# A two-layer transformer kernel on one core: new times for every piece of the schedule, and layer 1's middle rounds written out on all engines

## The reference

```python
# layer 0, attention: 16 heads of 16, rotary positions on q and k, causal mask
att = softmax(where(mask, q @ k.T / sqrt(16), -inf)); y = (att @ v) @ Wo.T + bo
# layer 0, feed forward: hidden 768, integer weights scaled by 1/127
out = (silu(x @ wg.T) * (x @ wu.T)) @ wd.T
# layer 1, attention: 16 heads of 64, clamped scores, causal mask
sim = 50 * tanh(q @ k.T / 8 / 50); y = (softmax(where(causal, sim, min)) @ v) @ Wo.T
# layer 1, channel mix: x mixed with the token before it
out = sigmoid(xr @ W_r.T) * (square(relu(xk @ W_k.T)) @ W_v.T)
```

## Time and profile before

| | us |
|---|---|
| median of 3 runs | 1533.23 |
| lowest and highest | 1530.34, 1533.83 |
| the profiled execution | 1535.46 |
| its span, first to last instruction | 1533.3 |
| PE, DVE, ACT, POOL busy in it | 1431.3, 1077.9, 800.4, 813.9 |

### The profile page before, as it was taken

How to read it: one execution, slowest core, us unless ns; L and a number is a source line. 1 busy time by engine, 2 the same in 40 slices (tenths; PEclk the granted TensorE clock), 3 DMA queues, 4 the chain that set the end, 5 groups by cost and what they waited for, 6 DMA issues and landing times. The chain is left out here.

```text
span 1533.3 us, 32896 instructions
## 1 busy us (share of the span) xinstructions
PE 1431.3 (93%) x12438; PEld 1053.3 (69%) x12438; DVE 1077.9 (70%) x2036; ACT 800.4 (52%) x1132; POOL 813.9 (53%) x1003
## 2 busy tenths in 40 slices
PE   5788989899999999999999999999999999999996
PEld 3555756667676767677777777777777777777765
DVE  7778687778887787785656658657677586675765
ACT  2443444353544443545656666665666566566651
POOL 4233434344443544344657567656666575756652
PEclk8888999899999999999999999999999999999999
DMA  5111120212121111220100001100100001000000
GB/s 189 60 59 53 48 82 22 84 43 83 41 83 41 55 55 62 78 70 16 48 29 1 1 4 40 42 1 1 43 1 15 29 1 42 1 1 29 1 29 14
DMA packets 45762, 61.32 MB, mean 40 GB/s; under 512 B 3760, under 2 KB 31312, under 8 KB 45648
## 3 DMA queue, kind: packets, MB, share of 16 engines
q1 hardware_dynamic: 44784, 59.03, 11.4%
q10 hardware_dynamic: 864, 0.66, 0.2%
HBM read 25.83 MB, written 8.39 MB: 22 GB/s over the span
## 5 line engine op out<-in xcount | busy, mean ns | idle before, releaser
L1696 ACT ACTIVATE l_probs<-psum 128x1024 f32<-128x1024 f32 (+1 forms) x192 | 164.4, 880 | 131.3 <-PE psum L1964 107.7
L912 ACT ACTIVATE l_probs<-psum 128x512 f32<-128x512 f32 x256 | 138.2, 595 | 179.0 <-PE psum L1179 176.6
L994 DVE TENSOR_REDUCE l_rowmax<-psum 128x2 f32<-128x1024 f32 (+2 forms) x192 | 159.2, 864 | 39.7 <-PE psum L1140 39.3
L310 POOL TENSOR_SCALAR_AFFINE_SELECT l_probs<-l_probs 128x256 f32<-128x256 f32 (+1 forms) x384 | 182.4, 506 | 0.0
L305 POOL TENSOR_TENSOR l_pool_holder<-expo 128x1 f32<-128x1 f32 x128 | 31.6, 247 | 282.7 <-ACT l_probs L1702 186.5
L1771 DVE TENSOR_TENSOR l_qk_lo<-psum,l_qk_hi 128x1024 fp32r<-128x1024 f32 x64 | 77.9, 1218 | 134.9 <-ACT l_qk_hi L1686 134.5
L1702 ACT ACTIVATE l_probs<-l_probs 128x2048 f32<-128x2048 f32 (+1 forms) x128 | 161.6, 1268 | 0.5
L2007 PE MATMUL psum<-l_probs,l_v 128*32 128x512 f32 (+3 forms) x2048 | 151.1, 434 | 0.7 <-DVE l_att L1793 0.7
L1780 DVE RECIPROCAL l_keysum<-psum 128x256 f32<-128x256 f32 x64 | 112.2, 1754 | 51.7 <-PE psum L1993 51.2
L1793 DVE TENSOR_TENSOR l_att<-psum,l_keysum 64x256 f32<-64x256 f32 x256 | 108.0, 422 | 20.3 <-PE psum L2007 13.0
L2007 PEld LDWEIGHTS psum<-l_probs,l_v 128*32 128x32 f32 x2048 | 64.2, 110 | 83.0 <-issue 71.4
(11 more groups left out here) (212 smaller groups left out, 4176.4 us busy)
## 6 DMA issues: line engine op xcount, KB each, us to landing
l_kT<-l_roped_hi SPq DMA_DIRECT2D x32, 256.0 KB, 2.5
l_qT<-l_roped_hi SPq DMA_DIRECT2D x32, 256.0 KB, 2.5
l_xin<-in_x SPq DMA_DIRECT2D x8, 512.0 KB, 4.4
l_kT<-l_roped_lo SPq DMA_DIRECT2D x16, 256.0 KB, 2.5
l_qT<-l_roped_lo SPq DMA_DIRECT2D x16, 256.0 KB, 2.5
l_x<-in_x SPq DMA_DIRECT2D x8, 512.0 KB, 4.0
x_mid<-l_x SPq DMA_DIRECT2D x8, 512.0 KB, 3.1
l_xin<-x_mid SPq DMA_DIRECT2D x8, 512.0 KB, 4.3
```

The source lines that it names most:

```text
L310: nc.gpsimd.affine_select(out=part, in_=part, compare_op=ALU.is_ge, fill=0.0, base=0, pattern=[[0, part.shape[1]], [1, P]], channel_multip ...
L912: space.free(nc.scalar.activation(probs[:, SLOT[p], e, c0:c1], space.unit(*use), ACT.Exp, scale=HD0 ** -0.5), *use)
L994: reduced = nc.vector.tensor_reduce(rowmax[:, a // 2, :, a % 2, t], space.unit("max", a, k)[:, :, c0:c0 + (t + 1) * P], mybir.AxisListType ...
L1696: space.free(nc.scalar.activation(probs[:, p % 2, :, c0:c1], space.unit("score", p, u)[:, :, 0:c1 - c0], ACT.Tanh, scale=HD1 ** -0.5 / CLA ...
```

## The change

Three things are changed, and no piece is added, removed or rewritten.

1. Every time in both layers' `table` and `moved_table`, in `loading_table` and in `prologue_table` is another one. The number of rounds between batches stays; the order within a round changes in places, on every engine.
2. A few banks change: in layer 0 those of `maxT`, `score`, `heat`, `warm`, `outT`, `o` and `x_T` in some indices, in layer 1 those of `end_heat`.
3. `loop()` of layer 1 is called with `unrolled=True`, so that ACT, DVE, POOL and SP also have rounds 3 to 6 written out. Layer 0 loops as before.

The core of the diff. Layer 0's loading, one moved line and one line of banks:

```diff
-        "rope_hi": {(0, 0): -20.101, (0, 1): 21.429, (0, 2): 46.819, (0, 3): 71.689, (1, 0): -15.688, (1, 1): 24.852, (1, 2): 50.682, (1, 7): 168, (2, 0): -14.54, (2, 1): 31.73, (2, 2): 54.28, (2, 7): 179.17, (3, 0): 6.041, (3, 1): 38.791, (3, 2): 56.891, (3, 7): 179.411},
+        "rope_hi": {(0, 0): -27.088, (0, 1): 22.112, (0, 2): 47.212, (0, 3): 71.998, (1, 0): -18.44, (1, 1): 25.56, (1, 2): 47.41, (1, 7): 168, (2, 0): -5.63, (2, 1): 27.82, (2, 2): 54.09, (2, 7): 173.94, (3, 0): 8.097, (3, 1): 36.997, (3, 2): 58.147, (3, 7): 178.927},
...
-        "load_lo": {(4,): -11.75, (5,): -11.68, (6,): -11.6, (7,): -7.78, (8,): -6.33, (9,): -2.17, (10,): 7.46, (11,): 12.9, (12,): 16.93, (13,): 40.62, (14,): 46.77, (15,): 52.09},
+        "load_lo": {(4,): -12.87, (5,): -12.68, (6,): -11.12, (7,): -8.66, (8,): -6.11, (9,): 2.47, (10,): 9.19, (11,): 14.74, (12,): 16.72, (13,): 42.7, (14,): 48.27, (15,): 49.3},
...
-        "maxT": {(0,): 7, (1,): 7, (2,): 3, (3,): 7},
+        "maxT": {(0,): 7, (1,): 1, (2,): 3, (3,): 7},
```

Layer 1's table, its loop and the banks of end_heat:

```diff
-        "mask": {(0,): 1.709, (1,): 4.13, (2,): 7.33, (3,): 15.022, (4,): 20.998, (5,): 23.104, (6,): 24.004, (7,): 24.419},
-        "sum": {(0,): 1.72, (1,): 5.051, (2,): 11.05, (3,): 17.267, (4,): 21.827, (5,): 23.106, (6,): 24.403, (7,): 24.75},
-        "den": {(0,): 10.961, (1,): 13.821, (2,): 14.411, (3,): 17.566, (4,): 18.315, (5,): 24.369, (6,): 27.23, (7,): 29.19},
-        "pv": {(0,): 10.965, (1,): 13.817, (2,): 15.513, (3,): 17.563, (4,): 20.735, (5,): 24.365, (6,): 27.317, (7,): 29.194},
-        "att": {(0,): 7.86, (1,): 11.991, (2,): 16.01, (3,): 20.46, (4,): 21.6, (5,): 23.95, (6,): 27.138, (7,): 27.672},
-        "att_lo": {(0,): 10.004, (1,): 14.2, (2,): 19.395, (3,): 21.864, (4,): 23.446, (5,): 25.464, (6,): 25.732, (7,): 28.856},
-        "x3_stats": {(): 36.047},
+        "mask": {(0,): 1.596, (1,): 5.23, (2,): 8.23, (3,): 15.242, (4,): 19.773, (5,): 23.27, (6,): 24.224, (7,): 24.565},
+        "sum": {(0,): 3.413, (1,): 5.71, (2,): 10.264, (3,): 16.351, (4,): 22.275, (5,): 23.75, (6,): 24.564, (7,): 25.219},
+        "den": {(0,): 10.736, (1,): 13.748, (2,): 14.424, (3,): 17.525, (4,): 18.15, (5,): 24.713, (6,): 26.994, (7,): 29.061},
+        "pv": {(0,): 10.74, (1,): 13.72, (2,): 15.264, (3,): 17.885, (4,): 20.828, (5,): 24.563, (6,): 26.998, (7,): 29.057},
+        "att": {(0,): 8.201, (1,): 12.828, (2,): 15.534, (3,): 20.61, (4,): 21.865, (5,): 23.77, (6,): 26.984, (7,): 28.08},
+        "att_lo": {(0,): 7.829, (1,): 13.242, (2,): 19.151, (3,): 22.505, (4,): 23.806, (5,): 25.39, (6,): 26.212, (7,): 28.768},
+        "x3_stats": {(): 36.814},
...
-        schedule.loop(eng, pieces, unrolled=eng.engine == nc.tensor.engine)
+        schedule.loop(eng, pieces, unrolled=True)
...
-        "end_heat": {(0,): 3, (1,): 1, (2,): 4, (3,): 0, (4,): 3, (5,): 3, (6,): 0, (7,): 2, (8,): 0},
+        "end_heat": {(0,): 5, (1,): 3, (2,): 5, (3,): 2, (4,): 5, (5,): 5, (6,): 5, (7,): 2, (8,): 0},
```

More of the change, by code:

```diff
@@ L530, in phase1 @@
[L530 to L536, removed]
@@ L539, in phase1 @@
[L539 to L542, removed]
@@ L551, in phase1 @@
[L551 to L563, removed]
@@ L578, in phase1 @@
-        "rmax_tail": {(0,): 6.953, (1,): 10.441, (2,): 16.277, (3,): 23.481},
-        "tail": {(0,): 13.301, (1,): 19.04, (2,): 27.248, (3,): 31.138},
-        "exp_tail": {(0,): 15.394, (1,): 21.24, (2,): 27.74, (3,): 32.72},
+        "load_x": {(): -22.958},
+        "x_stats": {(): -15.954},
+        "x_rstd": {(): -19.245},
+        "x_norm": {(): -14.007},
+        "x_T": {(0,): -12.79, (1,): -11.356},
+        "x_T_hi": {(0,): -12.4, (1,): -11.761},
+        "x_T_lo": {(0,): -12.722, (1,): -11.607},
@@ new lines, in phase1 @@
+        "outT_norm": {(0,): 20.075, (1,): 25.307, (2,): 32.112, (3,): 32.81},
+        "att_T": {(0,): 34.05, (1,): 34.051},
+        "att_T_hi": {(0,): 34.32, (1,): 34.668},
+        "att_T_lo": {(0,): 33.513, (1,): 33.517},
+        "o": {(0,): 34.93, (1,): 35.46},
+        "o_out": {(0,): 35.274, (1,): 35.364},
+        "x1_T": {(0,): 40.415, (1,): 40.849},
+        "x1_T_hi": {(0,): 43.53, (1,): 43.76},
+        "x1_T_lo": {(0,): 41.047, (1,): 41.051},
+        "o_stats": {(): 36.061},
+        "o_rstd": {(): 32.66},
@@ L581, in phase1 @@
+        "x2_rstd": {(): 55.15},
+        "x2_norm": {(): 56.26},
+        "x2": {(): 55.95},
+        "store": {(): 60.41},
+        "max_tail": {(0,): 5.265, (1,): 10.25, (2,): 16.367, (3,): 22.562},
+        "rmax_tail": {(0,): 7.07, (1,): 10.352, (2,): 16.54, (3,): 23.02},
+        "tail": {(0,): 13.219, (1,): 19.159, (2,): 27.326, (3,): 30.992},
+        "exp_tail": {(0,): 15.741, (1,): 20.885, (2,): 28.586, (3,): 31.05},
     }
@@ new lines, in phase2 @@
+        "x3_stats_b": {(): 45.213},
+        "x3_stats": {(): 36.814},
+        "x3_rstd_b": {(): 81.14},
+        "x3_rstd": {(): 37.011},
+        "x3_norm_b": {(): 51.044},
+        "x3_norm": {(): 37.211},
+        "x3_T_b": {(): 49.352},
+        "x3_T": {(): 39.254},
+        "x3_T_out_b": {(): 61.13},
+        "x3_T_out": {(): 39.13},
+        "mix": {(0,): 40.92, (1,): 41.882},
+        "mix_hi": {(0,): 40.313, (1,): 41.968},
+        "mix_lo": {(0,): 40.355, (1,): 43.577},
+        "r": {(): 41.948},
@@ new lines, in phase2 @@
+        "r_out": {(): 43.47},
+        "key": {(): 41.902},
+        "key_out": {(): 43.135},
+        "square": {(): 45.4},
+        "kact_hi": {(): 44.139},
+        "kact_lo": {(): 45.861},
+        "out": {(): 47.128},
+        "gate_b": {(): 56.408},
+        "gate": {(): 45.975},
+        "x4_stats_b": {(): 93.025},
+        "x4_stats": {(): 47.499},
+        "x4_rstd_b": {(): 91.854},
+        "x4_rstd": {(): 47.802},
+        "x4_norm_b": {(): 71.843},
+        "x4_norm": {(): 49.047},
@@ L1417, in phase2 @@
+        "store_b": {(): 82.102},
+        "store": {(): 41.32},
     }
```

414 lines of the change are left out of this document (194 added, 220 removed), and 15 rows, old and new, of the table moved_table.

## The result

The changed kernel takes 1536.93 us (median of 20 runs, 1533.38 to 1540.97) against 1533.65 for the kernel before (20 runs): a ratio of 1.0022, 95% interval 1.0012 to 1.0031. It is slower by 0.2%; forecast was 1524.2. The measured time lies in the range, on the other side of the kernel before.

What follows compares the result with a forecast made beforehand. PE, busy 93% of the span, was taken as the bound, with its idle time and low-clock stretches to win. Terms −2.0 − 3.0 − 0.4 − 4.6 + 0 + 0 + 1.0 = −9.0 gave 1524.2 us, range 1513 to 1539.

Steps and rivals of the forecast that it cites:

- Start of layer 0: Layer 0's start: moving load_lo.7 and load_lo.9 away from DVE's row-maximum reductions was to bring maxT.0 earlier, −2.0 us.
- Batch 1: Layer 0's start, rope_hi.3: an earlier split on ACT was to remove PE's 1.80 us wait for q's transfers, −3.0 us.
- The wait at 169.37: PE's 1.48 us wait for rmax behind a load_lo on DVE that moves away: −0.4 us.
- Layer 1's loop: Three PE waits in each looped round of layer 1 were to go: −1.15 us a round, −4.6 over four.
- All three waits: Layer 1's loop round: PE's two waits for POOL's key sum (0.6 us) and one for DVE before x3_T (0.6).
- The forecast for writing out: Layer 1's rounds written out on ACT, DVE, POOL and SP: 0 us, bounds −1.0 and +3.2.
- Layer 0's loop: PE's 1.17 us wait before rope.0 was to return as one idle block of about 1.9: 0 a round.
- End: Last batch: end_heat matmuls move behind out, so x3_T's transposes start at the lower clock for longer: +1.0 us, bounds 0 and +5.
- More low-clock time, the forecast's other side: Rival, layer 0's loop: an idle block before max.51 brings three low-clock stretches of 4.2 us each, total 1536.8; chance 0.13.
- The slack before den.0: Rival, layer 1's loop: slack falls from 4.4 to 0.4 us; if mask.0 comes later, PE waits, total 1539.6; chance 0.08.
- The forecast's own range: Whole kernel: the terms' own bounds, leaving out those that are rivals, give 1519 to 1530 us.

Runs made afterwards that it cites:

- `after_old_start`: The changed kernel with layer 0's rounds before its loop, the weight loading times and the warm banks as before: 1535.13 us, ratio 1.0010 to the kernel before.
- a mix 0.16% faster than before: Old start, layer 0 loop and end with the new passage and new layer 1 loop, written out: 1531.33 us, ratio 0.9984 to the kernel before.

## Why the prediction was wrong

**Start, the step that failed.** Forecast −2.0 − 3.0 − 0.4, measured +3.6 in the two traces and +6.2 in the mean of traces (x_T of the fourth batch at 206.3 in three new ones, at 200.2 in six old ones). Some 1.9 of it may be the new loop's place for x_T, by the one trace of `after_old_start` (203.93, before 202.08); that leaves +4.3. The priced moves do what they were priced at where they stand alone in the old order, the second in full, the first only up to maxT.0. What failed are the sentences in "Start of layer 0" and "Batch 1" that read a gain from the waits that go. The change moves all pieces of the start, and I had priced three. Unpriced were the fillers ahead of batch 0's products (the second pair of max pieces is 1.6 us later than with the load_lo move alone) and what the new order does to the clock around batch 1's maxima (3.9 us between the pv rows). The wait at 169.37 is gone whole, but from the second of these pv rows to x_T of the fourth batch it takes 48.9 us with the new start and loop against 48.1 before, so its −0.4 doesn't show either. Of the pair's +3.6, the 1.3 at the first max piece is the clock's first rise, which falls either way in one and the same start: chance, and no part of the change that the runs show. Which piece of the new start makes the stretch at 92 stays open. The kernel after does what I said at rope_hi.3: the split at 117.66 stands right behind v_out and ahead of the other evictions, and PE waits 0.77 for something else:

```profile
117.66 0.62 ACT L886 ACTIVATE l_roped_hi<-l_roped_lo 128x512 fp32r<-128x512 f32 x1
126.76 0.50 PE L1133 MATMUL psum<-l_kT,l_qT 63*128 63x512 f32 x2 [0.77 <-ACT l_probs L912]
```

But the rows there stand 5.6 us later than before (121.16), nearly all of it lost ahead of them.

**Layer 1's loop.** Forecast −1.15 a round, measured −0.46. All three waits went, as said; 0.3 came back as PE's wait for att before pv.0, 0.2 as its wait for ACT before scores, and PE's busy time rose by 0.24. The size was off by these terms. The forecast for writing out, 0 with a bound of +3.2, was right in the bound: +0.6 a round in the old order is near the +0.8 that the earlier trace rows show with the 100.00 of the written-out stretch, which I had set aside. No stall at the jump shows in the traces; most of either sign is the collision above. The Trainium skill ("Runtime: NRT & Kernel Launch", "Instruction fetch mechanics") says that kernels prefer unrolling where possible. The measured +2.4 for four rounds in the old order goes against that, the −1.6 in the new order with it.

**Passage between the layers.** Not priced, −1.9 in the pair and −2.0 in the mean: 309.5 to 311.2 us in eleven traces with the new times, 312.2 to 312.7 in nine with the old. It is, with layer 1's loop, the part of the change that is good. Which wait it saves was not looked for.

**Layer 0's loop.** Forecast 0, measured +0.2 in this pair, −0.5 in the mean of traces. The waits moved behind rope.0 as said, but into 0.90 and 0.50, not one block of 1.9.

**End.** Forecast +1.0 with heats from about 1526.7 for 7.1 us: measured wait 8.32, heats at 1527.82 for 7.09, +1.1 in the mean, +2.0 in this trace.

```profile
1505.19 2.02 PE L2035 MATMUL psum<-ident,l_xn 128*128 128x128 f32 x8 [8.32 <-DVE l_xn L423]
1527.82 7.09 PE L438 MATMUL psum<-l_wrkv_hi 128*128 128x512 f32 x30 [0.78 <-DVE l_xn L1873]
```

**Rivals.** More low-clock time, the forecast's other side, is what happened in kind (2.6 of 3.2 us go with the mean clock), but not at its place: in layer 0's loop both traces have the same 23.9 us of it. That its 1536.8 is so near the measured 1536.9 is luck. The slack before den.0 held with 0.2 us. The forecast's own range was also drawn too narrow by its own terms: its end at 1530 leaves out the +3.2 written down for the written-out rounds and most of the end's +5.

The stretches' means add to +2.9 (start with the loop's place for x_T +6.2, layer 0's loop −0.5, passage −2.0, layer 1 −1.9, end +1.1), and the runs say +3.2 by their means. Single traces scatter by 2 us and more, so each part's share is known only roughly.

## What to carry to other kernels

Where a change moves everything, a sum over the waits that vanish counts only one side: each removed wait needs the row of what stands at its place after, and each filler that moves ahead of a product is a term of its own. Before a microsecond in one trace is put down to an edit, look at other traces with the same code there: the 1.6 us by which the first max piece came earlier with another bank number come and go without it. Test the parts by swapping them between the two schedules, one time zone at a time; here that found a mix 0.16% faster than before in one step. And print the mean granted clock beside each time: inside one kernel it goes with most of the scatter.

## What the runs showed of the hardware

- Within one kernel, runs with 0.001 less mean granted clock take 1.0 us longer of 1535 (337 runs).
- In the same start PE runs its first real product at 0.40 or at 0.63 us a matmul, as it falls, and the first max piece is 1.3 us apart by that.
- DVE and POOL hold each other up: three selects 1.35 to 2.57 us, a sum over 128x768 1.84 to 2.70, and a DVE instruction on 128x4 from 0.17 to 1.32, until POOL's instruction of the same start is done.
- Writing a loop out changed a round by +0.6 or −0.4 us. 0.4 of the first stands beside such a collision, and so does a wait of 0.7 of PE that went with the second; no stall at the jump shows.
